# Turning softmax probabilities with VectorE and transfers inside SBUF in a sixteen-head attention and mixture-of-experts layer

## The reference

```python
q, k, v = (mxfp4_matmul(ln(x), w_codes, w_scales) + b  for q, k, v)   # 16 heads of 128
scores = einsum('bqhd,bkhd->bhqk', q, k) / sqrt(128)                  # 2048 x 2048 per head
out = einsum('bhqk,bkhd->bqhd', softmax(scores), v)
x = x + layernorm(mxfp4_matmul(out, wo_codes, wo_scales) + bo)
combine = top-2 of 8 experts of softmax(ln(x) @ Wr), renormalised
x = x + layernorm(sum_e combine_e * (silu(ln(x) @ Wg_e) * (ln(x) @ Wu_e)) @ Wd_e)
```

## Time and profile before

| | |
|---|---|
| median of 3 runs | 2777.99 us (2773.73 to 2778.16) |
| the profiled execution | 2775.19 us, span 2773.3 us |
| granted TensorE clock, mean | 0.974 of full |
| busy share of the span | TensorE 95%, weight loads 79%, VectorE 69%, ScalarE 52%, GpSimd 12% |
| first scores start, first turn of the last chunk | 52.1 us, 2473.9 us |
| attention ends, span ends | 2507 us, 2773 us |

### The profile page before, as it was taken

The page is one execution under the profiler, slowest core; times in us unless marked ns, Lnnn a source line. Parts: engine busy times, 40 slices in busy tenths (PEclk is TensorE's granted clock), DMA queues, the critical chain, the costliest instruction groups (busy, mean ns, idle before and its releaser), DMA issues.

```text
span 2773.3 us, 44497 instructions
## 1 busy us (share of the span) xinstructions
PE 2633.1 (95%) x14588; PEld 2189.6 (79%) x14588; DVE 1904.9 (69%) x3375; ACT 1454.4 (52%) x2924; POOL 332.2 (12%) x399
## 2 busy tenths in 40 slices
PE   4999999999999999999999999999999999996998
PEld 3788888888887888888888888888878888874876
DVE  4677767676776767676767777676767777775453
ACT  2565546464555646464555556464645555553332
POOL 1101010010101010100101010101001010004433
PEclk8999999999999999999999999999999999997999
DMA  5000000000000000000000000000000000020000
GB/s 107 8 5 12 5 6 12 2 16 2 12 5 13 5 13 5 4 14 2 16 2 12 5 13 5 13 5 2 16 2 16 2 5 1 1 83 11 8 9 16
DMA packets 52874, 34.23 MB, mean 12 GB/s; under 512 B 10080, under 2 KB 52448, under 8 KB 52448
## 3 DMA queue, kind: packets, MB, share of 16 engines
q1 hardware_dynamic: 52576, 30.59, 4.8%
HBM read 28.47 MB, written 2.10 MB: 11 GB/s over the span
## 4 chain that ended last, share of the span: by engine, by line
PE 91%; DVE 4%; issue 2%; DMA 1%; ACT 1%; SPq 1%; POOL 0%; POOLq 0%; DVEq 0%; ACTq 0%
PE ps_t L504 15%; PE ps_a L419 13%; PE ps_a L421 12%; PE ps_a L420 12%; PE ps_s L419 12%; PE ps_s L421 11%; PE ps_s L420 11%; DVE part_max L896 2%; DVE pT_lo L916 1%; DMA acc<-in_L_attn_bo 1%; PE ps_a L673 1%; PE ps_a L675 1%; PE ps_a L676 1%; PE ps_t L659 1%; ACT probs L712 1%
## 5 line engine op out<-in xcount | busy, mean ns | idle before, releaser
L721 ACT ACTIVATE pT_hi<-ps_t 128x512 fp32r<-128x512 f32 x1024 | 613.7, 599 | 776.5 <-PE ps_t L504 761.6
L916 DVE TENSOR_TENSOR pT_lo<-ps_t,pT_hi 128x512 fp32r<-128x512 f32 x1024 | 705.9, 689 | 329.4 <-ACT pT_hi L721 309.0
L712 ACT ACTIVATE probs<-ps_s,shift 128x512 f32<-128x512 f32 (+1 forms) x768 | 637.5, 830 | 302.7 <-DVE shift L910 302.7
L896 DVE TENSOR_REDUCE part_max<-ps_s 128x1 f32<-128x512 f32 (+1 forms) x768 | 663.4, 866 | 156.1 <-PE ps_s L421 146.6
L504 PEld LDWEIGHTS ps_t<-ident,probs 128*128 128x128 f32 x4096 | 512.6, 141 | 141.3 <-issue 9.2
L504 PE MATMUL ps_t<-ident,probs 128*128 128x128 f32 x4096 | 619.6, 274 | 0.8 <-ACT probs L712 0.8
L419 PE MATMUL ps_s<-kT_hi,qT_hi 128*128 128x512 f32 x1024 | 475.4, 464 | 45.9 <-issue 25.0
L419 PE MATMUL ps_a<-pT_hi,v_hi 128*128 128x512 f32 x1024 | 433.6, 423 | 34.0 <-DVE pT_lo L916 33.7
L421 PE MATMUL ps_s<-kT_hi,qT_lo 128*128 128x512 f32 x1024 | 413.2, 403 | 0.0
L420 PE MATMUL ps_s<-kT_lo,qT_hi 128*128 128x512 f32 x1024 | 412.3, 403 | 0.0
L421 PE MATMUL ps_a<-pT_hi,v_lo 128*128 128x512 f32 x1024 | 405.2, 396 | 0.0
(11 more groups left out here) (148 smaller groups left out, 3037.0 us busy)
## 6 DMA issues: line engine op xcount, KB each, us to landing
probs<-in_L_attn_x SPq DMA_DIRECT2D x4, 512.0 KB, 5.5
codes_k<-in_L_attn_wk_codes SPq DMA_DIRECT2D x16, 128.0 KB, 2.2
scales_k<-in_L_attn_wk_scales SPq DMA_DIRECT2D x64, 32.0 KB, 3.0
codes_q<-in_L_attn_wq_codes SPq DMA_DIRECT2D x16, 128.0 KB, 2.2
scales_q<-in_L_attn_wq_scales SPq DMA_DIRECT2D x64, 32.0 KB, 3.2
codes_v<-in_L_attn_wv_codes SPq DMA_DIRECT2D x16, 128.0 KB, 3.2
scales_v<-in_L_attn_wv_scales SPq DMA_DIRECT2D x64, 32.0 KB, 3.1
codes_o<-in_L_attn_wo_codes SPq DMA_DIRECT2D x16, 128.0 KB, 2.1
```

The source lines that it names most:

```text
L712: nc.scalar.activation(probs[:, j % 2, r, cols], ps_s[:, cols], ACT.Exp, bias=shift[:, j % 2, r:r + 1], scale=SCALE, accum_out=sums[:, j % ...
L721: nc.scalar.activation(pT_hi[:, k % RING, :], ps_t[:, k % 2, :], ACT.Copy).then_inc(sm["pt_hi"], 1)
L896: V.tensor_reduce(part_max[:, j % 2, r, part:part + 1], ps_s[:, slice(*MAX_PARTS[part])], AX.X, ALU.max)\
L916: V.tensor_tensor(pT_lo[:, k % RING, :], ps_t[:, k % 2, :], full(pT_hi[:, k % RING, :]), ALU.subtract)\
```

## The change

TensorE no longer turns the probabilities. They are turned in three steps.

1. exps writes its output in another order, so that the 32x32 blocks of a row lie together (blocks). It now works in two parts of 1024 keys.
2. VectorE turns each 32x32 block in place (turn, V.transpose), 128x1024 elements at a time. This is done as soon as the exponential of that part is there, in the same slot that makes the scores.
3. A transpose in blocks leaves each block in the wrong group of 32 partitions. SP therefore issues 16 transfers of 32 partitions x 4096 bytes from probs to a new tile pT in SBUF, for each half (8 key tiles) of a chunk (turn_blocks). They wait until weighted_values has used the same half of the chunk before.

After that, ScalarE copies a key tile from pT to pT_hi (SBUF to SBUF), and GpSimd, not VectorE, subtracts it from pT in place (probs_lo). The copy of key tile k is issued at position k + 10 of the stream of 16 positions a slot (HI_LAG), its product at position k + 12 (PV_LAG); before, the turn was at position k and the product at k + 2.

The six banks that are not ps_a become three pairs. The scores of a row are two parts of a pair each, and the pairs go round (pair_of). The four value projections all move to slot j = 0, their high part goes to ScalarE (value_hi) and their low part to VectorE (value_lo). The value bias is no longer added to the values: each head multiplies it with the output weights (bias_out) and adds the product up in vb_sum, which is added to acc at the end (finish_chunk). out_proj and add_out move one slot later. Codes and scales have one buffer for all four kinds, so the loads stand between the transfers of the probabilities in SP's order, and the weights between the subtractions in GpSimd's. In the last slot of the last head SP issues the loads of the mixture of experts, and x once more, ahead of the second half of the last chunk.

```diff
-    MAX_PARTS = [(0, HALF), (HALF, HALF + CH), (HALF + CH, S)]
-    EXP_PARTS = [(0, CH), (CH, HALF), (HALF, S)]
+    PAIRS = 3
+    USES = TPC * NG2
+    PV_LAG = 12
+    HI_LAG = 10
+    LOADS = Q4 * Q4 * 16
...
+        def key_at(h, j, pos, lag):
+
+            if pos >= lag:
+                return (h, j, pos - lag) if has(h, j) else None
+            if not has(h, j, -1):
+                return None
+            return ((h, j - 1) if j else (h - 1, NCH - 1)) + (pos + KT - lag,)
+
+        def blocks(j, g):
+
+            return probs[:, j % 2, :].rearrange("p (g j t r q) -> p g j t r q", g=NG2, j=Q4, t=GT, r=TPC)[:, g]
+
+        def pair_of(j, use):
+
+            return ((USES * (j - 1) if j else USES * (NCH - 1) + NCH) + use) % PAIRS
...
+            def turn_blocks(h, j, g):
+
+                m = NCH * h + j
+                wait(sp, "p_turned", USES * m + USES - NG2 + g + 1)
+                sp.sem_inc(sm["turn_seen"], 1)
+                wait(sp, "pv_done", KT * (m - 1) + GT * (g + 1))
+                for i in range(Q4):
+                    for b in range(Q4):
+                        sp.dma_start(full(pT[32 * b:32 * (b + 1), g, i, :, :]).rearrange("p t q -> p (t q)"),
+                                     blocks(j, g)[32 * i:32 * (i + 1), b].rearrange("p t r q -> p (t r q)"))\
+                            .then_inc(pT_loaded[g], 16)
...
+            def body(h):
+                last = isinstance(h, int) and h == H - 1
+                for j in range(NCH):
+                    if j == 0 and not last:
+                        wait(sp, w_ready["v"], h + 1)
+                        if isinstance(h, int) and h == 0:
+                            sp.wait_ge(w_ready["k"], 1)
+                        load("k", h + 1)
+                    turn_blocks(h, j, 0)
+                    if j == 2 and not last:
+                        wait(sp, w_ready["q"], h + 2)
+                        load("v", h + 1)
+                    if j == NCH - 1 and last:
+                        sp.wait_ge(pT_loaded[0], LOADS * (CHUNKS - 1))
+                        sp.wait_ge(pT_loaded[1], LOADS * (CHUNKS - 1))
+                        load_gate_up(0)
+                        sp.dma_start(d_raw[:, :, :],
+                                     wd.rearrange("e i n -> (e i) n").rearrange("(g p) n -> p g n", p=P))\
+                            .then_inc(d_loaded, 16)
+                        load_gate_up(1)
+                        load_gate_up(2)
+                        sp.wait_ge(sm["scores_ready"], USES * CHUNKS)
+                        for g in range(NCH):
+                            rows = slice(g * TPC, (g + 1) * TPC)
+                            sp.dma_start(x1[:, rows, :], xv[:, rows, :]).then_inc(res_loaded[g], 16)
+                    turn_blocks(h, j, 1)
+                    if j == 0:
+                        if not last:
+                            wait(sp, w_ready["k"], h + 2)
+                        load("o", h)
+                    if j == 1 and not last:
+                        wait(sp, w_ready["o"], h + 1)
+                        load("q", h + 1)
+
...
+            def probs_lo(h, j, k):
+                n = KT * (NCH * h + j) + k
+                g, t = k // GT, k % GT
+                wait(pool, "p_hi_done", n + 1)
+                tile = pT[:, g, :, t, :]
+                pool.tensor_tensor(tile, full(tile), full(pT_hi[:, k % RING, :]).rearrange("p (i q) -> p i q", i=Q4),
+                                   ALU.subtract).then_inc(sm["p_lo_done"], 1)
...
+                            if j == 0 and pos == 8 and not last:
+                                weights("k", h + 1)
+                            if j == 1 and pos == 8:
+                                weights("o", h)
+                            if j == 2 and pos == 0 and not last:
+                                weights("q", h + 1)
+                            if j == 3 and pos == 0 and not last:
+                                weights("v", h + 1)
+                        key = key_at(h, j, pos, HI_LAG)
+                        if key:
+                            probs_lo(*key)
...
+            def scores(h, j, r, g):
 
                 m = NCH * h + j
+                use = NG2 * r + g
+                if use == 0:
                     wait(pe, "q_lo", m + 1)
+                if j == 0 and r == 0:
+                    wait(pe, "k_lo", NCH * h + 2 * g + 2)
+                if j == 0 and use < PAIRS:
+                    wait(pe, "k_lo", NCH * h + use + 2)
+                else:
+                    wait(pe, "p_ready", USES * m + use - PAIRS + 1)
+                pair = pair_of(j, use)
+                for b in range(2):
+                    cols = slice((2 * g + b) * CH, (2 * g + b + 1) * CH)
+                    last = product3(ps_s[:, pair, b * CH:(b + 1) * CH], qT_hi[:, r * P:(r + 1) * P],
+                                    qT_lo[:, r * P:(r + 1) * P], kT_hi[:, cols], kT_lo[:, cols])
                 last.then_inc(sm["scores_ready"], 1)
...
-            def turn_probs(h, j, k):
-
-                n = KT * (NCH * h + j) + k
-                for a in range(TPC):
-                    last = nc.tensor.transpose(ps_t[:, k % 2, a * P:(a + 1) * P],
-                                               probs[:, j % 2, a, k * P:(k + 1) * P], ident[:, :])
-                last.then_inc(sm["t_ready"], 1)
...
+                wait(pe, "p_lo_done", n + 1)
+                out = ps_a[:, j % 2, :].rearrange("p (i q) -> p i q", i=Q4)
+                hi = pT_hi[:, k % RING, :].rearrange("p (i q) -> p i q", i=Q4)
+                product3(out, v_hi[:, k, :], v_lo[:, k, :], hi, pT[:, k // GT, :, k % GT, :],
...
+                        if r == 0:
+                            if j == NCH - 1 and has(h, j, 1):
+                                k_proj(h + 1, 0)
+                                k_proj(h + 1, 1)
                             key(0)
+                            if j == NCH - 1 and has(h, j, 1):
+                                k_proj(h + 1, 2)
+                                k_proj(h + 1, 3)
                             key(1)
                         if has(h, j, 1):
                             scores(*nxt, r, 0)
+                        if r:
+                            key(TPC * r)
+                        if r == 1 and has(h, j, -2):
+                            out_proj(h, j, 1)
+                        if r == 2 and j == 0 and has(h, j):
+                            v_proj(h, 1)
+                        if r == 2 and j == 2 and has(h, j):
+                            bias_out(h)
+                        if r:
+                            key(TPC * r + 1)
+                        if r == 0:
+                            key(2)
+                            if has(h, j, -2):
+                                out_proj(h, j, 0)
+                        if r == 3 and j == 0 and has(h, j):
+                            v_proj(h, 3)
                         if has(h, j, 1):
                             scores(*nxt, r, 1)
+                        if r == 3 and has(h, j, 2):
                             q_proj(*after)
+                        if r:
+                            key(TPC * r + 2)
+                        if r == 1 and j == 0 and has(h, j):
+                            v_proj(h, 0)
+                        if r == 2 and j == 0 and has(h, j):
+                            v_proj(h, 2)
                         key(TPC * r + 3)
...
+                out = blocks(j, g)[:, :, :, r, :].rearrange("p j t q -> p t j q")
+                src = ps_s[:, pair_of(j, NG2 * r + g), :].rearrange("p (t j q) -> p t j q", t=GT, j=Q4)
+                nc.scalar.activation(out, src, ACT.Exp, bias=shift[:, j % 2, r:r + 1],
+                                     scale=SCALE, accum_out=sums[:, j % 2, r, g:g + 1])\
                     .then_inc(sm["p_ready"], 1)
...
+                m = NCH * h + j
+                g, t = k // GT, k % GT
+                if t == 0:
+                    wait(act, pT_loaded[g], LOADS * (m + 1))
+
+                wait(act, "pv_done", KT * m + k - RING + 1)
+                nc.scalar.activation(pT_hi[:, k % RING, :].rearrange("p (i q) -> p i q", i=Q4), full(pT[:, g, :, t, :]),
+                                     ACT.Copy).then_inc(sm["p_hi_done"], 1)
...
+                        key(TPC * r)
+                        if r == 2 and j == 0 and has(h, j):
+                            value_hi(h, 1)
+                        if r == 3 and has(h, j, -1):
                             out_hi(h, j)
+                        key(TPC * r + 1)
+                        if r == 3 and j == 0 and has(h, j):
+                            value_hi(h, 3)
+                        key(TPC * r + 2)
+                        if r == 3 and has(h, j, 2):
+                            q_hi(*after)
                         if has(h, j, 1):
                             exps(*nxt, r, 0)
+                        if r == 1 and j == 0 and has(h, j):
+                            value_hi(h, 0)
```

(36 more changed lines are left out.)

449 lines of the change are left out of this document (187 added, 262 removed).

## The result

| | before | after |
|---|---|---|
| median | 2777.72 us (4 runs) | 2842.03 us (4 runs, 2830.41 to 2857.39) |
| ratio, 95% interval | | 1.0241 [1.0197, 1.0284] |
| profiled execution, span | 2775.19, 2773.3 us | 2834.33, 2832.5 us |
| granted TensorE clock | 0.974 | 0.943 |
| first scores to end of the last exponential | 52.1 to 2473.74: 2421.6 us | 51.8 to 2495.84: 2444.0 us |

The account below looks back on a forecast made before the run. TensorE's issue order bounds the kernel before; afterwards a chain of waits returns nearly all the time taken from TensorE. Span 2762 plus 77 for the clock is 2839, plus 4.7 to the median: 2844 us, 2.4% slower; range 2650 to 3200.

Parts of the forecast that it names:

- The round: Ordinary row: exponential, copy, subtraction, weighted values, scores, maximum, shift, next exponential wait in turn, 7.05 us; TensorE's work 5.6.
- Row 0: First row of a chunk: scores(0,0), VectorE's maximum, turn and add_out stand ahead of the next exponential, 10.1 us.
- the two-pass rival: VectorE's turn takes two passes, 2.3 us, making VectorE late: 397 us more, 3240 us; chance 0.11.
- The loop's turn: Once a head, the turn of the loop over heads adds 3 us, as in the kernel before.
- The late load of q: Slot 2: GpSimd waits for q's loads, issued behind a half's transfers; tile 16's low part is late by 4.0 us.
- The transfers: SP's 2 MB half: issuing 7.3 us, last landing 2 to 3 later; 11.7 us taken, hidden with 2.8 to spare.
- The end: From the turns of the last chunk to the last moments: 60 us, 25 more than before.
- The clock: TensorE idles 1.8 us in each row 0, then runs at half speed: 1.2 us each, 77 us in all.
- The first rival: The chain of waits holds but TensorE's clock does not fall: 2767 us, 0.4% faster; chance 0.20.
- the transfers' rival: A half takes longer than 14.5 us, each us past that costing 64 us: at 20 us, 3190 us; chance 0.09.
- the one in which the clock falls in every row: Half speed on TensorE in three more rows, 4.5 us a chunk, 288 us more: 3130 us; chance 0.10.
- the one in which TensorE never waits: Low parts arrive before TensorE needs them, all 451 us kept: 2352 us, or up to 2650 if partly; chance 0.14.

Follow-up runs that it names:

- copy_first: Changed kernel with ScalarE's copy at position 4r+3 issued ahead of exps(r, 0), not behind it: 2741.25 us, ratio 0.9897 to the kernel before.
- sub_chain: Changed kernel with one more GpSimd subtraction ahead of every fourth tile's (k % 4 == 1), all but last head: 3219.08 us, ratio 1.1635 to the kernel before.
- sub_off: Changed kernel with one more GpSimd subtraction ahead of tiles k % 4 == 3, all but last head: 2868.23 us, ratio 1.0367 to the kernel before.
- no_turn: Changed kernel with each VectorE turn cut to its first 32 of 1024 columns (output wrong): 2755.04 us, ratio 0.9961 to the kernel before.
- straight: Changed kernel with a half's 16 transfers replaced by four of 512 KB within their partitions (output wrong): 2720.76 us, ratio 0.9814 to the kernel before.
- combo4: Changed kernel with ScalarE's copy earlier; q_hi, q's weights, last loads, add_out, one VectorE turn and TensorE's tile 2 later: 2473.78 us, ratio 0.8951 to the kernel before.

## Why the prediction held, step by step

- **The round.** Worked out as 7.05 us, measured as 7.01 to 7.02. copy_first shows that it is this round (a single copy moved out of it shortened row 2 to what was worked out), sub_chain that a term of it counts in full (1.24 for a subtraction of 1.29), sub_off that the same outside it counts for little. A chunk was to be 31.8 and is 31.81 (row 1 0.13 shorter than worked out, row 3 0.16 longer). The 451 us taken from TensorE do come back as waiting.
- **Row 0** was to be 10.1 and is 10.04 to 10.12. The path that I summed, through VectorE's turn, is the later one by 0.25 only. The prediction names the work of the other, TensorE's own, but does not add it up; that it lies so close I learned from no_turn.
- **Durations without a row.** The turn: 1.23 taken, 1.235 measured, so the two-pass rival falls. Copy 0.622, 0.626. Subtraction 1.285, 1.289: neither GpSimd nor VectorE reads slower beside the other.
- **Slot 0 and keys.** 10.5 and 4.2 were to be added. 10.91 + 14.25 in slot 0 (its row 3 without a low stretch) is 10.5 over ordinary rows; keys 4.3.
- **The loop's turn, 3 us: wrong.** Row 0 of slot 0, in which it lies, is 10.12, 0.08 over the other. It lies beside the round.
- **The late load of q, 4.0 us: mis-sized.** It is 6.5 to 9.0 without the clock, 7.5 in the mean. Most of the error is SP's issue: 0.457 each from loads out of HBM, 10.02/16 = 0.63 for these transfers, so 16 of them put the loads 2.7 us later. The rest was not taken apart. This error and that of the loop's turn nearly cancel: a head without low stretches is some 150.5 us, predicted 150.4.
- **The transfers.** A half takes 11.9, 11.7 was taken. The two parts were not as said: issuing takes 10.0 and not 7.3, and the last transfer lands 2.5 behind the start of its issue. Hidden, in the main: ScalarE does wait for a half inside a head, some 24 us in all, where the prediction says none. But straight, which has none of these waits, has the same rows except the one with q. The Trainium skill's page "SBUF — State Buffer" (Door 1) gives about 218 GB/s for 32 partitions, because they reach 8 of the 16 ports. The trace, with 206 GB/s over 32 partitions and 407 over 128, does not contradict it, but since the issues alone would give 209, it does not show that the ports are what limits.
- **The end** was to be 60 us and is 69.5. Counted from the end of the last exponential: the first half of the last chunk is issued until 16.5 (12.8 predicted), the loads until 30.1 (25.4), the second half lands at 46 (40). SP's issues again, 11.83 for the last half and not 7.3. The 3.5 left are behind it, from eight tiles to the moments; there the mean clock is 0.72:

```profile
2541.80:2565.30 23.50, 11.81 (x42) 8.65 (x42) 9.80 (x30) 6.60 (x10) 13.26 (x13) 0.72 0.08 19
```

- **The clock: size nearly right, place wrong.** I had a low stretch in each row 0, 4.8 us a head. There is none: 10.04 to 10.13 in 14 heads, at 1.00. It falls in the wait for the weights of q (5.7 to 8.3 us), around or behind the 2.20 for out_lo in slot 0 in 12 of 15 heads and, in six heads, in slot 1, where the three idles ahead of it are at most 1.5. From the spread (16.36 against 14.25, 9.20 against 8.62) and the half-speed part behind the wait for q (TensorE is busy 3.78 us at 0.50 in it, so 1.9) it costs 2.1 + 0.6 + 1.9 = 4.6 a head, and 4.0 when the 0.6 is taken off, which the shorter wait for q gives back. I had read 1.8 us of idle as enough, since 1.74 and 2.05 were the earlier trace rows. But behind the 1.74 TensorE works only 3.22 of the next 6.00 us, so that row does not speak of the idle alone. (Nor did the clock stay full for 1.8 us behind the 2.05: it was low from 1.1 us on.) In the rows here a single idle of 1.65 leaves the clock full in every head. One of 2.20 does so in three heads and not in twelve, and one of 2.55 in one row of sub_chain and not in another. The length of the last idle is thus not all that decides; what else does, no run isolated.
- **The sum.** 2762 + 77 was to be the span; it is 2832.5. While scores are made: predicted 36 less for the order and 77 more for the clock, measured 22 more, so some 20 less than predicted. The end: 25 predicted, 36 measured. That 2844 stands beside 2842 is in part luck: these errors cancel, and the clock's size was nearly right, though its places were not foreseen.

The first rival (the clock does not fall) is excluded by 0.943; the transfers' rival by straight; the one in which the clock falls in every row by the ordinary rows of 7.02 us at 1.00; the one in which TensorE never waits by the round. But its place was named rightly: combo4, whose order takes the waits away, runs at 2474, inside the 2352 to 2650 given for it.
